# First attention: both halves' logits in a row, the values' products behind them, ScalarE's turned copies between the second half's exponentials

## The chip, the cores and the metric

The kernel runs on one core of a Trainium2 chip. The core has a matmul engine (TensorE, PE in the profile; its weight loads are shown apart as PEld), VectorE (DVE), ScalarE (ACT), GpSimd (POOL) and SyncE (SP), which issues most of the transfers. Each engine takes its own instructions in the order in which they are written, and waits for the others on semaphores. The metric is the device time of one execution in microseconds (us); lower is better.

## The reference

A small vision tower over 16 images of 36 patches and one class token each, so 37 tokens per image, 592 in all, 256 features wide, float32 throughout. Six stages follow each other: patch embedding, a first attention, a mixture of experts, a second attention with three iterations, and a feed-forward stage with quantised weights. The change is in the first attention alone:

```python
q = (x @ Wq.T + bq) * 16 ** -0.5          # 16 heads of 16
kv = x @ Wkv.T + bkv                       # one key and one value head for all
k, v = kv[..., :16], kv[..., 16:]
qr = q.reshape(B, 16 * 37, 16)
probs = softmax(qr @ k.T, axis=-1)         # (B, 592, 37)
out = (probs @ v)  # laid back to (B, 37, 256)
h = h + out @ Wo.T + bo
```

## The kernel before

The whole kernel is written as one instruction stream per engine. The 16 images are treated in two halves `u` of eight images. For each half the first attention goes through these steps:

- Logits: `attention_scores(u)` on TensorE (L1944) fills four banks `("S", u, j)`, one for each two images. A product has 16 rows of contraction and 37 columns, and four of them lie side by side in the array. 80 matmul instructions make one half.
- Softmax: `scores(u, j)` on VectorE takes the maximum (L1263) and writes logits less maximum into `probs`, which lies in the tile `big` (L1264); that empties the bank. `exps(u, j)` on ScalarE takes the exponential in place (L798). `row_sums(u, j)` on VectorE sums and inverts (L1270, L1271). GpSimd multiplies by the inverse (L629) and counts up `probs_ready`.
- Turning: TensorE's `probs_turned(u)` waits for all four multiplications of the half and turns the probabilities by 15 matmuls with the identity into five banks `("PT", u, t)` (L1958). They are copied to `probsT[u]`, which is `cur` for half 0 and `probs` for half 1: half 0 by ScalarE (L803), half 1 by ScalarE and VectorE in turn (L803, L1276).
- Output: `attention_values(u)` on TensorE (L1975, 128 matmuls) waits for all five copies and for `vals_ready`. ScalarE's `heads_out` (L808) takes the result to `att`, and `project` (L1756) multiplies by the output weights.

The values themselves come from `values_of_tokens()` on TensorE (24 matmuls into the bank `("v0",)`, recorded at L1756 as `bank<-wkvT,xT`), `values()` on VectorE (L1293 to L1298), which adds the bias, and `values_by_slot()` on GpSimd (L618), which spreads them over slots and counts up `vals_ready`.

There are eight PSUM banks, and they are used strictly in turn. The list `fills()` names every filling of a bank in TensorE's order, and who empties it. TensorE may fill number n only when number n - 8 is emptied. Emptied banks are counted by one semaphore for each emptying stream (`act`, `dve`, `rates`), in the order of that engine's work, and `NTH` gives the count that a key has to wait for. So the list has to have the same order as the engine's program, within each semaphore.

Before the change TensorE's order in this stage is: logits of half 0, values' products, logits of half 1, turn half 0, outputs of half 0, turn half 1, first part of the projection, outputs of half 1, rest of the projection. ScalarE's order is: four exponentials of half 0, four of half 1, five copies of the turned half 0, `heads_out` of half 0, and so on. VectorE's is: four `scores` of half 0, `values()`, four `row_sums` of half 0, four `scores` of half 1, four `row_sums` of half 1. GpSimd's is: four multiplications of half 0, `values_by_slot()`, four multiplications of half 1.

Of the kernel before, what the change touches and what calls it, by code (L numbers as in the profile page):

```python
# [26 lines left out]
ALU = mybir.AluOpType  # L27
# [3 lines left out]
P = 128  # L31
B = 16
NG = 6
T = NG * NG + 1
# [15 lines left out]
RT = 5  # L50
# [40 lines left out]
def fills():  # L91

    def channel(c, gs=range(2)):
        f.extend((("xp", 2 * c + half, g), "act") for g in gs for half in range(2))

    f = [(("ln",), "act")]
    f.extend((("ad", t), "act") for t in range(TT))
    channel(0)
    f.append((("cs",), "act"))
    channel(1, (0,))  # L100
    f.append((("mr",), "act"))
    f.append((("cr",), "dve"))
    channel(1, (1,))
    channel(2)
    f.append((("rt",), "rates"))
    f.extend((("y", t), "dve") for t in range(TT))
    f.append((("wl",), "dve"))
    f.append((("wn",), "dve"))
    f.append((("bl",), "dve"))
    f.append((("bq",), "act"))  # L110
    f.extend((("wT", n), "act") for n in ("q0", "o0"))
    f.append((("wkvT",), "act"))
    for i in range(3):
        f.append((("xT", 0, i), "act"))
    f.append((("k0",), "dve"))
    for g in range(6):
        f.append((("q0", g), "act" if g % 2 else "dve"))
    for u in range(2):
        f.extend((("S", u, j), "dve") for j in range(4))
        if not u:  # L120
            f.append((("v0",), "dve"))
    for u in range(2):
        f.extend((("PT", u, t), "act" if u == 0 or t % 2 == 0 else "dve") for t in range(RT))
        if u:
            f.append((("wo", 0, 0), "dve"))
        f.extend((("PV", u, g), "act") for g in range(2))
    f.extend((("wo", 0, j), "dve") for j in range(1, 3))
    f.extend((key, "act") for key in (("pw", 0), ("wc", "q"), ("pw", 1), ("wc", 1), ("wc", 2), ("wc", 3), ("cst",)))
    for i in range(3):
        f.append((("xT", 1, i), "act"))  # L130
    f.extend((("lg", c), "act") for c in range(2))
    f.append((("lgT",), "act"))
    for e in range(NX + 1):
        if e < NX:
            for c in range(2):
                f.append((("g", e, c), "act"))
                f.append((("u", e, c), "dve"))
        if 1 <= e <= NE or e == NX:
            for i in range(3):
                f.append((("d", min(e - 1, NE), i), "dve"))  # L140
    f.extend((("fw", n), "dve" if n % 2 else "act") for n in range(6))
    f.extend((("wT", n), "act") for n in ("v1", "o1"))
    for i in range(3):
        f.append((("xT", 2, i), "dve" if i == 1 else "act"))
    us = range(2)
    f.extend((("nc", "k", 1, u), "act") for u in us)
    for u in us:
        f.append((("nc", "q", 1, u), "dve"))
        f.append((("nv", 1, u), "act"))
    f.extend((("nc", "k", 2, u), "act") for u in us)  # L150
    f.extend((("vt", u), "act") for u in us)
    for a in (1, 2, 3):
        f.append((("fS", a, 0), "dve"))
        f.append((("fV", a), "act"))
        f.append((("fS", a, 1), "dve"))
        if a == 1:
            f.extend((("vr", 0, j), "dve") for j in range(4))
            f.extend((("vr", 1, j), "act" if j < 2 else "dve") for j in range(4))
        else:
            f.extend((("out", a - 1, u), "act") for u in us)  # L160
        f.extend((("fPT", a, u), "act") for u in us)
        if a == 1:
            f.extend((("nv", 2, u), "act") for u in us)
        if a == 1:
            f.append((("nc", "k", 3, 0), "act"))
        if a == 3:
            f.append((("df",), "dve"))
        f.extend((("O", a, u), "dve") for u in us)
        if a == 1:
            f.append((("nc", "k", 3, 1), "act"))  # L170
        f.extend((("OT", a, u), "dve") for u in us)
        if a < 3:
            f.extend((("nc", "q", a + 1, u), "dve") for u in us)
        if a == 1:
            f.extend((("nv", 3, u), "act") for u in us)
    f.extend((("out", 3, u), "dve") for u in us)
    for i in range(3):
        f.append((("wo", 1, i), "dve"))
    f.extend((("fw", n), "act") for n in range(6, 9))
    for i in range(3):  # L180
        f.append((("xT", 3, i), "dve" if i == 1 else "act"))
    f.extend((("ga", o, c), "act") for o in range(FC) for c in range(2))
    f.append((("mx", 1), "dve"))
    f.extend((("up", c), "act") for c in range(len(UC)))
    f.extend((("mx", n), "dve") for n in (2, 3, 4))
    f.extend((("dn", t), "dve") for t in range(TT))
    return f
# [8 lines left out]
ROOTS.extend(("placed", _t) for _t in range(TT - 2, TT))  # L196
ROOT = {key: n + 1 for n, key in enumerate(ROOTS)}
NTH = {}
for _who in ("act", "dve", "rates"):
    for _n, _key in enumerate(k for k, w in FILLS if w == _who):  # L200
        NTH[_key] = (_who, _n + 1)

# [7 lines left out]
def build(nc, i, out):  # L210

    with ExitStack() as ctx:
# [3 lines left out]
        def sem(name):  # L216
            return ctx.enter_context(nc.semaphore(name))
# [180 lines left out]
        banks = [ctx.enter_context(nc.psum_tensor(f"bank{n}", [P, 512], F32)) for n in range(8)]  # L398

        bank_filled = sem("bank_filled")  # L400
        emptied_by = {"act": sem("act_emptied"), "dve": sem("dve_emptied"), "rates": sem("rates_emptied")}
        dve_chain, act_chain, pool_chain = sem("dve_chain"), sem("act_chain"), sem("pool_chain")
        images_in = [sem(f"images_in{n}") for n in range(NC)]
        (patch_w_in, ln_in, norm_rows_in, cols_in, small_w_in, attn_w_in, rows_in, pos_in, moe_in, ffn_in, out_stored) = (
# [139 lines left out]
        def _(pool):  # L544
# [68 lines left out]
            def values_by_slot():  # L613

                pool.wait_ge(attn_cleared, 3)
                pool.wait_ge(values_in, 1)
                for h_ in range(2):
                    ins = pool.tensor_tensor(vals[0:G3, :, :, h_, h_ * HD:(h_ + 1) * HD],  # L618
                                             vb[:, :, :].unsqueeze(2).to_broadcast([G3, 6, 3, HD]),
                                             slot_of[:, :].unsqueeze(1).unsqueeze(3).to_broadcast([G3, 6, 3, HD]), ALU.mult)  # L620
                ins.then_inc(vals_ready, 1)

            for u in range(2):
                if u:
                    values_by_slot()
                for j in range(4):
                    pool.wait_ge(sums_ready, 4 * u + j + 1)
                    v = probs[:, u, :, 2 * j:2 * j + 2, :]
                    pool.tensor_tensor(v, v, row_sum[:, u, j].unsqueeze(3).to_broadcast([P, RT, 2, T]),  # L629
                                       ALU.mult).then_inc(probs_ready, 1)  # L630
            filled(pool, ("wo", 0, 2))
            pool.memset(att[:, :], 0.0).then_inc(attT_cleared, 1)

# [59 lines left out]
        def _(act):  # L693
# [101 lines left out]
            def exps(u, j):  # L795
                emptied(act, ("S", u, j))
                v = probs[:, u, :, 2 * j:2 * j + 2, :]
                act.activation(v, v, ACT.Exp).then_inc(exp_done, 1)  # L798

            def probs_turned(u, t):  # L800
                b = take(act, ("PT", u, t))
                n = min(P, R - t * P)
                empty(act.copy(probsT[u][:, :, t * P:t * P + n], b[0:G3, 0:3 * P].rearrange("p (g r) -> p g r", g=3)[:, :, 0:n]))  # L803
# [6 lines left out]

            for j in range(4):
                exps(0, j)
            for j in range(4):
                exps(1, j)
            for t in range(RT):
                probs_turned(0, t)
            for g in range(2):
                heads_out(0, g)
            for t in range(0, RT, 2):
# [192 lines left out]
        def _(dve):  # L1012
# [275 lines left out]
            def values():  # L1288

                b = take(dve, ("v0",))[:, 0:6 * HD].rearrange("p (u g d) -> p u g d", u=2, g=3)  # L1290
                bv = bv_row[:, :].unsqueeze(1).unsqueeze(1)
                v = vb.rearrange("p (u g) d -> p u g d", u=2)
                link(dve.memset(vb[64:G3, :, :], 0.0))  # L1293
                link(dve.tensor_tensor(v[:, :, 0:2, :], b[0:G3, :, 0:2, :], bv[0:G3].to_broadcast([G3, 2, 2, HD]), ALU.add))
                ins = dve.tensor_tensor(v[0:2 * T, :, 2, :], b[0:2 * T, :, 2, :],
                                        bv_row[0:2 * T, :].unsqueeze(1).to_broadcast([2 * T, 2, HD]), ALU.add)
                empty(ins)
                dve.tensor_copy(first[:, 0:1], ident[0:T, 0:1]).then_inc(values_in, 1)  # L1298

            for j in range(4):  # L1300
                scores(0, j)
            values()
            for j in range(4):
                row_sums(0, j)
            for j in range(4):
                scores(1, j)
            for j in range(4):
                row_sums(1, j)
# [423 lines left out]
        def _(pe):  # L1732
# [258 lines left out]
            for g in range(6):  # L1991
                emptied(pe, ("q0", g))
            attention_scores(0)
            values_of_tokens()
            attention_scores(1)

            probs_turned(0)
            attention_values(0)
# [284 lines left out]
```

## Time and profile before

| what | value |
|---|---|
| time, median of three runs | 292.12 us (292.08 to 292.67) |
| the profiled execution's own time | 292.1 us |
| its span, first to last instruction | 290.4 us |
| mean granted TensorE clock over the span | 0.929 of full |
| PE busy, DVE busy, ACT busy, POOL busy | 88%, 70%, 35%, 20% |
| the first attention, from its first logits to the end of its projection | 52.5 to 83.9 us |

The profiled execution is a normal one: its time lies inside the three runs. 1.7 us of it lie outside the span. The rows of the next section come from this execution; all places in them are microseconds from the span's start.

### The profile page before, as it was taken

The numbers are of one execution on the slowest core, as the hardware profiler recorded it, in microseconds if no ns is written. First come the engines' busy times: TensorE is split into PE (matmuls) and PEld (weight loads), VectorE is DVE, ScalarE is ACT, GpSimd is POOL, SyncE is SP. The second block draws the span as 40 slices with busy tenths as digits, with TensorE's granted clock in tenths as the row PEclk, the third lists the DMA queues.
The fourth block names the chain that finished last, engine by engine and source line by source line (L and its number), as shares of the span: only waits on it lengthen the run. The fifth ranks groups of instructions, "written<-read, shape, count | busy, mean of one in ns | idle before, by whom it ended". The sixth has DMA issues, their size and how long they took to land.

```text
span 290.4 us, 5610 instructions
## 1 busy us (share of the span) xinstructions
PE 254.6 (88%) x2199; PEld 208.9 (72%) x2199; DVE 201.9 (70%) x483; ACT 101.1 (35%) x243; POOL 58.4 (20%) x117
## 2 busy tenths in 40 slices
PE   5999989896999999999999799988788999745696
PEld 4888879795986677877777587866566776434584
DVE  2884866487532697888979667856878548987831
ACT  2571352115325511111112564672304337444000
POOL 8770540054012000000000144992000000000000
PEclk9988979757899999999999999999899999969599
DMA  7949540000005300000000000000000000000011
GB/s 202 270 129 282 154 166 5 2 2 2 2 2 180 146 2 0 0 0 2 0 1 0 2 0 2 3 0 2 2 3 0 0 0 2 0 0 1 0 36 47
DMA packets 14471, 12.01 MB, mean 41 GB/s; under 512 B 2995, under 2 KB 13902, under 8 KB 14446
## 3 DMA queue, kind: packets, MB, share of 16 engines
q1 hardware_dynamic: 14376, 11.62, 13.5%
q8 instruction: 17, 0.28, 0.4%
q10 hardware_dynamic: 70, 0.05, 0.1%
q14 instruction: 8, 0.07, 0.1%
HBM read 11.05 MB, written 0.61 MB: 40 GB/s over the span
## 4 chain that ended last, share of the span: by engine, by line
PE 70%; DVE 18%; ACT 7%; issue 3%; POOL 1%; ACTq 0%; DVEq 0%; POOLq 0%
PE bank L1756 46%; PE bank L1838 5%; PE bank L2250 5%; PE bank L1911 3%; PE bank L1944 3%; DVE part L1600 2%; PE bank L1975 2%; PE bank L1751 2%; DVE big L1664 1%; DVE keys_n L1645 1%; PE bank L1886 1%; DVE big L1698 1%; ACT big L1002 1%; PE bank L1783 1%; ACT xT L776 1%
## 5 line engine op out<-in xcount | busy, mean ns | idle before, releaser
L1756 PE MATMUL bank<-xT,big 128*128 128x296 f32 (+1 forms) x192 | 45.7, 391 | 0.0
L1756 PEld LDWEIGHTS bank<-xT,big 128*128 128x128 f32 x192 | 34.3, 190 | 9.5 <-issue 0.2
L1756 PE MATMUL bank<-xT,fT 128*128 128x296 f32 (+12 forms) x96 | 24.6, 416 | 0.6 <-DVE xT L1621 0.6
L853 ACT ACTIVATE cen<-bank 128x296 f32<-128x296 f32 x20 | 8.3, 418 | 46.4 <-PE bank L1756 40.7
L1756 PE MATMUL bank<-big,cur 128*128 128x256 f32 (+1 forms) x100 | 23.3, 381 | 0.7 <-DVE cur L1375 0.7
L1751 PE MATMUL bank<-ident,ones 128*128 128x128 f32 x104 | 18.0, 340 | 5.3 <-POOL rsd L559 3.5
L1756 PEld LDWEIGHTS bank<-xT,fT 128*128 128x128 f32 x96 | 17.2, 191 | 7.1 <-issue 2.1
L1756 PEld LDWEIGHTS bank<-big,cur 128*128 128x128 f32 (+1 forms) x100 | 18.0, 182 | 4.9 <-DVE cur L1375 1.5
L1751 PEld LDWEIGHTS bank<-ident,ones 128*128 128x128 f32 x104 | 16.8, 249 | 5.8 <-POOL rsd L559 3.5
L1388 DVE SCALAR_TENSOR_TENSOR h<-bank,route,h 128x256 f32<-128x256 f32 (+1 forms) x40 | 17.0, 478 | 2.9 <-PE bank L1756 2.9
L669 POOL TENSOR_SCALAR big<-keys_n,k_w 128x256 f32<-128x256 f32 x24 | 17.5, 748 | 4.8 <-DVE keys_n L1479 4.8
L1600 DVE TENSOR_REDUCE part<-big 128x1 f32<-128x296 f32 (+2 forms) x18 | 13.1, 731 | 6.3 <-ACT big L989 6.3
L661 POOL COPY cur<-xT 128x256 f32<-128x256 f32 x2 | 0.7, 402 | 72.3 <-ACT xT L778 72.3
L2250 PE MATMUL bank<-fT,big 128*128 128x256 f32 (+1 forms) x60 | 14.7, 410 | 0.5 <-DVE big L1597 0.5
L1838 PE MATMUL bank<-small,big 128*128 128x256 f32 (+1 forms) x60 | 14.9, 415 | 0.0
L2250 PEld LDWEIGHTS bank<-fT,big 128*128 128x128 f32 (+1 forms) x60 | 11.9, 201 | 3.2 <-DVE big L1597 0.8
L1838 PEld LDWEIGHTS bank<-small,big 128*128 128x128 f32 (+1 forms) x60 | 12.0, 202 | 2.4
L1375 DVE TENSOR_TENSOR cur<-cen,bank 128x296 f32<-128x296 f32 x20 | 9.1, 461 | 4.8 <-PE bank L1756 4.4
L1756 PE MATMUL bank<-wT_o,att 128*128 128x256 f32 (+1 forms) x40 | 9.3, 383 | 1.5 <-DVE att L1556 0.9
L629 POOL TENSOR_TENSOR big<-big,row_sum 128x370 f32<-128x370 f32 x8 | 6.2, 811 | 20.6 <-DVE row_sum L1271 20.6
L2220 PE MATMUL bank<-ident,mx 128*128 128x128 f32 x4 | 1.7, 422 | 9.4 <-DVE mx L1603 5.6
L1756 PEld LDWEIGHTS bank<-wT_o,att 128*128 128x128 f32 (+1 forms) x40 | 7.0, 182 | 3.1 <-DVE att L1556 1.3
(325 smaller groups left out, 514.9 us busy)
## 6 DMA issues: line engine op xcount, KB each, us to landing
big<-in_x SPq DMA_DIRECT2D x3, 576.0 KB, 7.6
big<-in_L_ffn_w_gate SPq DMA_DIRECT2D x2, 512.0 KB, 6.8
big<-in_L_ffn_w_up SPq DMA_DIRECT2D x2, 512.0 KB, 6.8
big<-in_L_ffn_w_down SPq DMA_DIRECT2D x1, 1024.0 KB, 5.5
small<-in_L_tok_lin_w SPq DMA_DIRECT2D x3, 256.0 KB, 5.4
small<-in_L_ffn_w_gate SPq DMA_DIRECT2D x1, 768.0 KB, 4.6
small<-in_L_ffn_w_up SPq DMA_DIRECT2D x1, 768.0 KB, 6.9
small<-in_L_ffn_w_down SPq DMA_DIRECT2D x1, 768.0 KB, 8.2
```

What stands on the lines that cost most here:

```text
L629: pool.tensor_tensor(v, v, row_sum[:, u, j].unsqueeze(3).to_broadcast([P, RT, 2, T]), ALU.mult).then_inc(probs_ready, 1)
L669: ins = pool.tensor_scalar(fkeys[a - 1][:, u, :, n, :], keys, k_w[:, a - 1, n:n + 1], 1.0, ALU.mult, ALU.mult)
L853: empty(act.activation(silu[:, c, :], b[:, 0:HP], ACT.Silu))
L1375: empty(dve.tensor_tensor(hid[:, e % 3, c * HP:(c + 1) * HP], silu[:, c, :], b[:, 0:HP], ALU.mult))
L1388: ins = dve.scalar_tensor_tensor(out=v, in0=src, scalar=route[0:n, t, e:e + 1], in1=v, op0=ALU.mult, op1=ALU.add)
L1600: return dve.tensor_reduce(part[:, n:n + 1], v, AX.X, ALU.max, apply_absolute_value=True)
L1751: pe.matmul(b[:, 0:P], ones[:, :], ident[:, :], start=True, stop=True)
L1756: ins = pe.matmul(out_, a_, b_, start=(n == 0), stop=(n == len(pairs) - 1))
L1838: ins = pe.matmul(b[0:rows, 0:D], patT[:, k, t * P:t * P + rows], lin_w[:, k, :], start=(k == 0), stop=(k == PK - 1))
L1911: ins = pe.matmul(b[32 * j:32 * j + m, at_:at_ + 4 * T].rearrange("p (u c) -> p u c", u=2), w(k), xq[:, k, :, 2 * j * T:2 * (j + 1) * T], ...
L1944: ins = pe.matmul(bs_[j][:, (2 * t + s) * T:(2 * t + s + 1) * T], qT[rows, row:row + P], kT[rows, u, s * T:(s + 1) * T], start=True, stop= ...
L2250: ins = pe.matmul(b[0:rows, 0:D], gate[:, o * NT + t * P:o * NT + t * P + rows], fT[2][:, o, :], start=(o == 0), stop=(o == FC - 1))
```

## The change

TensorE makes the logits of both halves without a break and the values' products after them. VectorE does the sums of half 0, two of the second half's `scores`, then `values()`, then the other two `scores`. GpSimd spreads the values after the four multiplications of half 0, as before, but this is now written out. ScalarE puts the five copies of the turned half 0 between the four exponentials of half 1. The bank of the values gets a semaphore of its own (`values`), because the place of `values()` in VectorE's program is no longer the place of its bank in the order of fills. The number of instructions that compute stays as it was on every engine.

```diff
@@ fills()
-    for u in range(2):
-        f.extend((("S", u, j), "dve") for j in range(4))
-        if not u:
-            f.append((("v0",), "dve"))
+    f.extend((("S", u, j), "dve") for u in range(2) for j in range(4))
+    f.append((("v0",), "values"))
@@ GpSimd
-            for u in range(2):
-                if u:
-                    values_by_slot()
-                for j in range(4):
-                    ...
+            for j in range(4):
+                normalised(0, j)
+            values_by_slot()
+            for j in range(4):
+                normalised(1, j)
@@ ScalarE
             for j in range(4):
                 exps(0, j)
-            for j in range(4):
-                exps(1, j)
-            for t in range(RT):
-                probs_turned(0, t)
+            exps(1, 0)
+            probs_turned(0, 0)
+            exps(1, 1)
+            probs_turned(0, 1)
+            probs_turned(0, 2)
+            exps(1, 2)
+            probs_turned(0, 3)
+            exps(1, 3)
+            probs_turned(0, 4)
@@ VectorE, values()
-                empty(ins)
+                ins.then_inc(emptied_by["values"], 1)
@@ VectorE
             for j in range(4):
                 scores(0, j)
-            values()
             for j in range(4):
                 row_sums(0, j)
-            for j in range(4):
+            for j in range(2):
+                scores(1, j)
+            values()
+            for j in range(2, 4):
                 scores(1, j)
             for j in range(4):
                 row_sums(1, j)
@@ TensorE
             attention_scores(0)
+            attention_scores(1)
             values_of_tokens()
-            attention_scores(1)
```

## Rows read from the trace of the kernel before

**Rows 1.** The page: share of the chain by engine.

```profile
PE 70%; DVE 18%; ACT 7%; issue 3%; POOL 1%; ACTq 0%; DVEq 0%; POOLq 0%
```

**Rows 2.** The chain that ended last, 51 to 92 us: start, length, what.

```profile
64.11 0.54 DVE row_max L1263
...
68.32 0.52 ACT big L798
68.84 1.78 ACT cur L803 x5
70.61 0.24 issue
70.85 3.82 PE bank L1975 x128
```

**Rows 3.** TensorE's timeline: start, length, what, times, idle before and who ended it.

```profile
55.46 4.18 PE L1756 MATMUL bank<-wkvT,xT 128*111 128x16 f32 x24
59.57 4.50 PE L1944 MATMUL bank<-kT,qT 16*128 16x37 f32 x80
64.57 3.48 PE L1958 MATMUL bank<-ident,big 128*111 128x128 f32 x15 [0.50 <-POOL big L629]
70.85 3.82 PE L1975 MATMUL bank<-cur,small 111*32 111x74 f32 x128 [2.80 <-ACT cur L803]
74.60 1.93 PE L1958 MATMUL bank<-ident,big 128*111 128x128 f32 x15
76.37 1.89 PE L1756 MATMUL bank<-wT_o,att 128*128 128x256 f32 x8
78.19 2.27 PE L1975 MATMUL bank<-probs,small 111*32 111x74 f32 x128
```

**Rows 4.** Windows: stretch, length, busy time of PE, PEld, DVE, ACT, POOL, granted clock, transfers.

```profile
51.40:54.20 2.80, 1.67 (x60) 1.70 (x61) 0.46 (x1) 0.51 (x1) 0.00 (x0) 1.00 0.03 6
54.30:67.80 13.50, 13.00 (x144) 12.73 (x141) 10.74 (x28) 3.59 (x7) 4.37 (x6) 0.50 0.00 1
67.90:71.20 3.30, 0.50 (x22) 0.38 (x25) 2.88 (x9) 2.28 (x6) 2.14 (x3) 1.00 0.00 0
71.40:74.60 3.20, 3.20 (x107) 3.00 (x100) 0.00 (x0) 0.41 (x1) 0.78 (x2) 0.50 0.03 5
...
190.80:194.20 3.40, 2.26 (x38) 1.59 (x37) 2.05 (x5) 2.11 (x9) 3.39 (x7) 1.00 0.00 0
194.20:197.60 3.40, 2.80 (x68) 2.16 (x68) 3.25 (x7) 2.29 (x10) 3.40 (x5) 1.00 0.02 5
```

**Rows 5.** VectorE's timeline around the two halves' softmax.

```profile
59.13 0.54 DVE L1264 TENSOR_TENSOR big<-bank,row_max 128x370 f32<-128x370 f32 x1
...
60.35 0.52 DVE L1270 TENSOR_REDUCE row_sum<-big 128x10 f32<-128x370 f32 x1
...
62.84 0.22 DVE L1271 RECIPROCAL row_sum<-row_sum 128x10 f32<-128x10 f32 x1
64.08 0.54 DVE L1263 TENSOR_REDUCE row_max<-bank 128x10 f32<-128x370 f32 x1 [1.02 <-PE bank L1944]
...
67.74 0.55 DVE L1264 TENSOR_TENSOR big<-bank,row_max 128x370 f32<-128x370 f32 x1
68.20 0.53 DVE L1270 TENSOR_REDUCE row_sum<-big 128x10 f32<-128x370 f32 x1
```

**Rows 6.** ScalarE's timeline, same stretch.

```profile
68.32 0.52 ACT L798 ACTIVATE big<-big 128x370 f32<-128x370 f32 x1 [0.52 <-DVE big L1264]
68.74 1.86 ACT L803 COPY cur<-bank 111x384 f32<-111x384 f32 x5
```

**Rows 7.** GpSimd's timeline, same stretch.

```profile
61.20 3.12 POOL L629 TENSOR_TENSOR big<-big,row_sum 128x370 f32<-128x370 f32 x4 [17.15 <-DVE row_sum L1271]
64.28 1.29 POOL L618 TENSOR_TENSOR small<-vb,slot_of 111x288 f32<-111x288 f32 x2
69.06 3.12 POOL L629 TENSOR_TENSOR big<-big,row_sum 128x370 f32<-128x370 f32 x4 [3.49 <-DVE row_sum L1271]
```

More of the change, by code:

```diff
@@ L198 @@
 NTH = {}
-for _who in ("act", "dve", "rates"):
+for _who in ("act", "dve", "rates", "values"):
     for _n, _key in enumerate(k for k, w in FILLS if w == _who):
@@ L400, in build @@
         bank_filled = sem("bank_filled")
-        emptied_by = {"act": sem("act_emptied"), "dve": sem("dve_emptied"), "rates": sem("rates_emptied")}
+        emptied_by = {"act": sem("act_emptied"), "dve": sem("dve_emptied"), "rates": sem("rates_emptied"),
+                      "values": sem("values_emptied")}
         dve_chain, act_chain, pool_chain = sem("dve_chain"), sem("act_chain"), sem("pool_chain")
@@ L621, in values_by_slot, with normalised @@
                 ins.then_inc(vals_ready, 1)
-            for u in range(2):
-                if u:
-                    values_by_slot()
-                for j in range(4):
[L627 to L630, printed above, removed]
+            def normalised(u, j):
+                pool.wait_ge(sums_ready, 4 * u + j + 1)
+                v = probs[:, u, :, 2 * j:2 * j + 2, :]
+                pool.tensor_tensor(v, v, row_sum[:, u, j].unsqueeze(3).to_broadcast([P, RT, 2, T]),
+                                   ALU.mult).then_inc(probs_ready, 1)
+            for j in range(4):
[3 more added lines that the diff above has]
+                normalised(1, j)
             filled(pool, ("wo", 0, 2))
```

## The prediction

> **What bounds the kernel now.** I read the page first: TensorE holds most of the chain that ended last [rows 1]. That is a mean over six stages, so I went to the chain in the first attention [rows 2]. There TensorE does not set the end throughout. At 64.11 the chain leaves it for VectorE, which takes the second half's maxima and subtractions until ScalarE has its last exponential at 68.32. Then come ScalarE's five copies of the turned half 0 to 70.61, and only then TensorE's outputs of half 0 at 70.85. TensorE's timeline shows the hole from its own side: its turning ends at 68.05, and it sits idle 2.80 us until ScalarE's copies are there [rows 3]. The bank copied first was full near 65.5 (three of the fifteen transposes), and ScalarE took it at 68.74 [rows 6]. ScalarE was not short of time: it idled 0.52 us before its last exponential, and its own order kept the copies behind it [rows 6].
>
> The granted clock comes next [rows 4]. From 54.3 to 67.8 it is 0.50, the level of 1.2 GHz: logits, values' products and turning. From 67.9 to 71.2 it is 1.00, 2.4 GHz, and there TensorE works only 0.50 of 3.30 us. From 71.4 to 74.6 it is 0.50 again, and TensorE works all of it. So the outputs of half 0 take 3.82 us, and the same 128 instructions for half 1, at full clock, 2.27 us [rows 3]. Ahead of the rise stood the transposes of half 0; ahead of the fall the hole.
>
> **The change part by part.**
>
> *TensorE: logits together, values' products last.* The two pieces that change places fill 55.46 to 64.07 without a hole, at half clock throughout [rows 3, 4]. In either order they are done by about 63.9; I take no gain and no loss (bounds 63.8 and 64.1). The logits of half 1 are then ready near 60.0, where VectorE waited 1.02 us for them until 64.08 [rows 5]. All eight banks are in use, so turning copies 3 and 4 now wait for the first two `scores` of half 1 (63.3 and 64.3, below), and are reached at 65.9 and later. That costs nothing.
>
> *VectorE.* `values()` costs 0.76 us: 1.22 us from the last subtraction (59.13) to the first sum (60.35), less the 0.46 us between such instructions where nothing is between them (67.74 to 68.20) [rows 5]. New order: sums of half 0 from 59.59, four in 2.62 us (60.35 to 63.06, less a small overlap), to 62.21. One `scores` is 4.12 / 4 = 1.03 us (64.08 to 68.20). Two of them reach 64.27, `values()` 65.03, two more 67.09. The sums of half 1 thus start 1.11 us sooner than at 68.20. Their cover: the values' products must be full by 64.3 and are at about 63.9. Past that margin of 0.4 us each tenth goes into all that follows.
>
> *GpSimd.* Half 0's multiplications come 0.76 us sooner, 60.44 to 63.56. The first transpose began 0.25 us after their end (64.32 to 64.57) [rows 3, 7], which gives 63.81. TensorE is free at about 63.9, so turning half 0 starts at 63.9 in place of 64.57. `values_by_slot()` now stands in front of half 1's multiplications with its wait for `values()`: 65.1 to 66.4 (1.29 us), while their first sum comes near 67.9. It has 1.5 us of cover, and the outputs need it only at 68.3. Half 1's multiplications come with VectorE, 1.11 us sooner: 67.95 to 71.07.
>
> *ScalarE.* A copy follows a copy after 0.37 us (1.86 for five), an exponential (0.52 us) is followed by a copy after 0.42 us [rows 6]. The transposes are 3.48 / 15, about 0.22 us apart and 0.42 us long, so the banks are full at 64.8, 65.4, 66.1, 66.7, 67.4. The `scores` of half 1 are done at 63.3, 64.3, 66.1, 67.2. In ScalarE's order: exponential 0 at 63.4, copy 0 at 64.8, exponential 1 at 65.2, copy 1 at 65.6, copy 2 at 66.1, exponential 2 at 66.5, copy 3 at 66.9, exponential 3 at 67.3, copy 4 at 67.7 to 68.1. With the 0.24 us of issue [rows 2] the outputs of half 0 start at 68.3 in place of 70.85. The copies now block exponentials in one queue. Queued behind exponential 3 are VectorE's fourth sum of half 1 (due 67.09 + 3 * 0.65 = 69.0) and behind that GpSimd. Exponential 3 ends at 67.8, so 1.2 us hide it.
>
> *What the earlier outputs gain.* They start where the clock was at full. Turning half 0 is still the work ahead of 67.8 (63.9 to 67.3 in place of 64.57 to 68.05), so I let the clock rise there as before. Outputs of half 0: 68.3 + 2.27 = 70.6. Turning half 1 then waits for GpSimd: 71.07 + 0.25 = 71.3 in place of 74.60. This is the term that counts, 3.3 us. The hole does not vanish: some 0.7 us of it now stands in front of that turning, and GpSimd's chain (VectorE's sums, in the end the `scores`) is late next.
>
> *Bounds on the outputs.* At half clock they take at most 3.82 us [rows 3] and end at 72.1. At full clock they are 2.27 us and hidden by the wait for GpSimd. I take 2.27.
>
> *After 71.3.* Turning half 1 takes 1.77 us to the projection (74.60 to 76.37), its first tenth at half clock; I take 0.1 us off. This needs full clock past 71.3, where it fell before. Before the fall TensorE had worked 0.50 of 3.30 us. Now it works some 2.3 of the same stretch. The nearest rows: 190.8 to 194.2, with 2.26 of 3.40 us of work and a hole of 1.2 us, and the clock stayed full to 197.6; against 51.4 to 54.2, with 1.67 of 2.80 us, all of it 16-row logits, and the clock fell [rows 4]. The outputs are like the first in share and in shape (32 array columns, as that stretch's logits and products have), so I take full clock.
>
> Everything later (projection, expert weights' composition, routing, experts) hangs on TensorE's chain and moves as a block, transfers of the last stage's weights with it, since they are issued on a bank of that chain. The new semaphore adds no instruction that computes: 0.
>
> Sum: 3.3 + 0.1 = 3.4 us off a span of 290.4 is 287.0; the profiled execution's 292.1, which is the median of the runs shown, becomes 288.7 us.
>
> *A rule against it.* The rows show the clock rise from 0.50 to 1.00 at about 67.8, with TensorE on nothing but the transposes of half 0 since 64.57 [rows 3, 4]. The Trainium skill, "TensorE: Matmul & The Clock Gate", section "Part 4: PE-mode transpose", says that the full clock doesn't engage for transposes. By that rule the outputs of half 0 would run at half clock, and the sum would be that of rival 2; the trace disagrees, as the clock rose right behind them.
>
> **Rivals.**
>
> 1. *The clock falls at 71.3 after all.* For: it fell exactly there before, and TensorE still has two holes in the stretch, of 0.5 and 0.7 us. Against: [rows 4] as above. Turning half 1 then takes about 3.48 in place of 1.93 us [rows 3]: gain 3.4 - 1.55 = 1.85, 290.3 us. If it stays down into the projection, up to 1.7 us more is lost (eight products of 1.89 us at full clock), which ends within measurement of no change.
>
> 2. *The clock does not rise at 67.8*, because turning ends 0.5 us before it now. Outputs end at 72.1, and turning half 1 starts at 72.15. At full clock: gain 2.45, 289.7 us. At half: 1.55 less, 291.2 us.
>
> 3. *ScalarE's queue becomes the bound; the change hardly does what it says.* If turning half 0 comes over 1.2 us later than 63.9, each copy holds an exponential and VectorE's sums with it. At 2 us late, GpSimd and turning half 1 are 0.8 us late, outputs run into the stretch after 71.3, and the gain is some 1.5 us: 290.6 to 291.6 us. For: one queue, four new places of waiting on TensorE. Against: the margins above.
>
> 4. *Slower: half clock over dense work.* A fall that is not lifted soon, as from 54.3 to 67.8 [rows 4], over the dense projection and compositions behind 71.3. Half clock takes twice the time of full, so each microsecond of it costs half a microsecond. It decides from 6.8 us of half clock on, where 3.4 us are lost; 13.5 us of it as there cost 6.75, which gives 292.1 - 3.4 + 6.75 = 295.4 us. Against: after 71.4 dense work at half clock brought full clock by 74.8.
>
> **How the numbers follow.** Forecast 0.62 (own range 288.2 to 289.2), rival 1 0.18, rival 2 0.07, rival 3 0.08, rival 4 0.05. The range goes from 287.9 (PE, VectorE and GpSimd bounds all at their good end, 0.8 us better) to 290.9 (rival 1 and a little more); outside are rival 4, most of rival 3, the bad end of 2, some 0.15 together. A measurement of this kernel can tell about 0.2%, 0.6 us. Faster by more: 0.62 + 0.18 + 0.06 + 0.04 = 0.90. Within: 0.05, from rivals 1, 2 and 3 at their ends. Slower: 0.05, rival 4.
>
> **What would show it.** In the profile after: logits of half 1 right behind half 0's and VectorE without a wait before 64; `values()` near 64.3 without a wait; ScalarE's last copy ending near 68.1; outputs of half 0 at 68.3 in about 2.3 us; turning half 1 near 71.3, released by GpSimd; granted clock 1.00 from 67.9 on. Wrong if TensorE's outputs of half 0 take near 3.8 us, if turning half 1 takes 3.5 us, if ScalarE waits for TensorE with exponentials behind it and VectorE waits for ScalarE, or if a new stretch at half clock stands later than 75.

## The result, and the profile after

| kernel | median | range | runs | ratio to the kernel before, 95% interval |
|---|---|---|---|---|
| before | 292.5 us | 291.95 to 294.8 | 20 | |
| changed | 289.38 us | 288.61 to 292.1 | 20 | 0.9894 [0.9872, 0.9915] |

Medians and ranges here are over all runs, while the ratios leave out the few runs of later batches that lie over 1.5% above the fastest of their kernel. The change makes the kernel 3.1 us faster (292.5 less 289.38), 1.1%; the interval of the ratio stands for 2.5 to 3.7 us. The forecast was 288.7 us against 292.1, which is 3.4 us less. The profiled execution of the changed kernel is one of its slower ones, 291.87 us with a span of 290.1: only 0.2 us less than before. So there are two things to read: the first attention, where the gain has to be, and what lies behind it.

TensorE's timeline of the changed kernel in the first attention (start, length, what, times, idle before and who ended it; compare [rows 3]; lines have moved by a few numbers):

```profile
52.66 7.17 PE L1953 MATMUL bank<-kT,qT 16*128 16x37 f32 x160 [1.15 <-ACT qT L793]
59.76 4.18 PE L1765 MATMUL bank<-wkvT,xT 128*111 128x16 f32 x24
63.86 3.51 PE L1967 MATMUL bank<-ident,big 128*111 128x128 f32 x15
68.30 2.27 PE L1984 MATMUL bank<-cur,small 111*32 111x74 f32 x128 [0.93 <-ACT cur L805]
71.30 1.86 PE L1967 MATMUL bank<-ident,big 128*111 128x128 f32 x15 [0.73 <-POOL big L625]
73.00 1.89 PE L1765 MATMUL bank<-wT_o,att 128*128 128x256 f32 x8
...
77.67 2.83 PE L1765 MATMUL bank<-wT_o,att 128*128 128x256 f32 x12 [0.56 <-ACT att L810]
```

The reader should see three things. The outputs of half 0 start at 68.30 in place of 70.85 and take 2.27 us in place of 3.82. Turning half 1 starts at 71.30 in place of 74.60, and GpSimd released it. The rest of the projection starts at 77.67, where the kernel before has 81.04 (an entry of its TensorE timeline of the same shape, `x12`): 3.37 us gained. ScalarE's timeline shows why the outputs could start:

```profile
63.36 0.51 ACT L800 ACTIVATE big<-big 128x370 f32<-128x370 f32 x1 [3.09 <-DVE big L1271]
64.85 0.48 ACT L805 COPY cur<-bank 111x384 f32<-111x384 f32 x1 [0.97 <-PE bank L1967]
65.22 0.52 ACT L800 ACTIVATE big<-big 128x370 f32<-128x370 f32 x1
65.64 0.97 ACT L805 COPY cur<-bank 111x384 f32<-111x384 f32 x2
66.50 0.52 ACT L800 ACTIVATE big<-big 128x370 f32<-128x370 f32 x1
66.92 0.47 ACT L805 COPY cur<-bank 111x384 f32<-111x384 f32 x1
67.28 0.53 ACT L800 ACTIVATE big<-big 128x370 f32<-128x370 f32 x1
67.69 0.36 ACT L805 COPY cur<-bank 111x240 f32<-111x240 f32 x1
```

From the first copy on ScalarE works without a hole, and the last copy ends at 68.05 in place of 70.60 [rows 6]. VectorE never waits for a logit of half 1 and starts its sums at 67.08 in place of 68.20 [rows 5]. GpSimd follows it to 71.05.

To compare executions a mark inside the stage is needed. VectorE's first maximum serves, since it is the first thing that VectorE does with the logits. The kernel before, then the changed one:

```profile
55.48 0.54 DVE L1263 TENSOR_REDUCE row_max<-bank 128x10 f32<-128x370 f32 x1 [3.62 <-PE bank L1944]
55.52 0.54 DVE L1270 TENSOR_REDUCE row_max<-bank 128x10 f32<-128x370 f32 x1 [3.54 <-PE bank L1953]
```

From there to the rest of the projection the kernel before takes 25.56 us (55.48 to 81.04) and the changed one 22.15 us (55.52 to 77.67), 3.4 us less.

The windows of the same execution (columns as in [rows 4]) show where the gain was lost again:

```profile
54.30:67.80 13.50, 13.07 (x150) 12.68 (x145) 11.69 (x31) 5.50 (x13) 4.40 (x6) 0.51 0.00 1
68.20:71.20 3.00, 2.27 (x128) 2.12 (x128) 1.49 (x6) 0.82 (x2) 2.85 (x4) 1.00 0.02 5
71.40:74.60 3.20, 3.20 (x23) 2.93 (x23) 2.29 (x4) 1.32 (x3) 0.00 (x0) 1.00 0.00 0
88.70:91.90 3.20, 3.02 (x6) 0.79 (x7) 0.00 (x0) 0.88 (x4) 0.84 (x5) 0.50 1.02 353
163.80:167.00 3.20, 3.20 (x17) 3.20 (x17) 0.00 (x0) 0.47 (x1) 0.37 (x2) 0.50 0.00 0
```

The granted clock rises ahead of the outputs and no longer falls behind them. But two new stretches at half clock (0.50) stand at 88.7 and 163.8. What they cost can be read off the same instructions in both kernels. The first two rows are of the kernel before, the other two of the changed one:

```profile
92.24 2.32 PE L1756 MATMUL bank<-xT,gate_w 128*8 128x320 f32 x8 [0.64 <-ACT xT L776]
165.53 2.05 PE L1756 MATMUL bank<-xT,wT_k 128*128 128x128 f32 x16 [1.07 <-ACT xT L778]
```

```profile
88.88 3.85 PE L1765 MATMUL bank<-xT,gate_w 128*8 128x320 f32 x8 [0.63 <-ACT xT L778]
163.52 3.61 PE L1765 MATMUL bank<-xT,wT_k 128*128 128x128 f32 x16 [0.92 <-ACT xT L780]
```

The router's logits took 1.53 us more and the second attention's first key products 1.56 us more. That is 3.1 us, nearly the whole gain. Idle time before them is the same or less, so nobody made them wait; they ran slower. In this execution the two stretches hide the change. Of the 20 runs 12 lie at 288.6 to 289.6 us, five at 290.5 to 291.0 and three, this one among them, at 291.8 to 292.1; what the clock did in the others was not recorded place by place.

### The profile page after: what moved, and what is told of

Its sections match the earlier page's. It is cut to its first block, busy times and chain, and to the rows that moved or that the text cites. A ratio compares the mean times of both kernels' runs of the same rounds, so it can differ in the third digit from the quotient of the medians.

```text
span 290.1 us, 5610 instructions
## 1 busy us (share of the span) xinstructions
PE 255.3 (88%) x2199; PEld 208.9 (72%) x2199; DVE 201.7 (70%) x483; ACT 100.9 (35%) x243; POOL 58.5 (20%) x117
## 4 chain that ended last, share of the span: by engine, by line
PE 67%; DVE 21%; ACT 6%; issue 3%; POOL 2%; ACTq 0%; DVEq 0%; POOLq 0%
PE bank L1765 46%; PE bank L2259 5%; PE bank L1847 5%; PE bank L1920 3%; DVE part L1609 2%; PE bank L1760 2%; DVE big L1271 1%; DVE big L1673 1%; DVE row_max L1270 1%; DVE keys_n L1654 1%; POOL big L625 1%; PE bank L1895 1%; PE bank L1953 1%; DVE big L1707 1%; ACT big L1009 1%
```

## The experiments

All medians below are of one batch each; the kernel before was run beside each of them. "Changed kernel" is the base for all variants but two, which start from the kernel before. Since the granted clock falls at other places from one execution to the next, a profile is read by the distances inside it, and the time by the ratio and its interval.

**The changed kernel again.**

> The changed kernel once more, as the base of this batch. Both theories: a gain of 3.1 us by the median. If the gain at the first attention (3.4 us) is fixed and the rest varies with where the granted clock falls later, the profile shows turning of half 1 at 71.3 us again, and the span lies at 287.0 plus about 1.5 us for each stretch at half clock between 85 and 204 us. If instead the late loss is fixed work added by the change, those stretches are there in every profile and the span is 290.1 again.

Measured: median 289.55 us, ratio 0.9915 [0.9879, 0.9951]. Its profile has a span of 287.8 us, where the expected sum (287.0 and 1.5 for one stretch) gives 288.5. Turning of half 1 again starts 3.01 us after the outputs of half 0 (67.51 to 70.52). The places are 0.8 us earlier than in the first profile, so the expected 71.3 was met only as a distance. Of the two late stretches only the second is there: the router's logits ran at full clock (2.32 us), the key products at half.

```profile
L1765 PE MATMUL bank<-xT,wT_k x16: 414/421/422, 161.2 to 164.4; 128*128 128x128 f32 x16
```

(Nanoseconds shortest/median/longest of one, first and last start; at full clock a key product takes 275 ns.) A third time, as the base of the last batch:

> The changed kernel a third time, as the base of this batch: median 289.4 to 289.6 us, turning of half 1 3.0 us after the start of the outputs of half 0.

Measured: median 289.51 us, ratio 0.9921 [0.9882, 0.996]; 68.52 to 71.52 is again 3.00 us. Here neither of the two late stretches occurred: the key products took 275 ns.

```profile
L1765 PE MATMUL bank<-xT,wT_k x16: 274/275/352, 162.2 to 164.0; 128*128 128x128 f32 x16
```

But the clock was at half elsewhere, from 203.8 to 207.2, over products of the second attention's last iteration. The same products in the kernel before, then in this execution (at full clock they take 2.02 us, as in the changed kernel's first profile):

```profile
207.07 3.04 PE L1756 MATMUL bank<-small,fprobsT 128*32 128x128 f32 x64
203.76 3.60 PE L1765 MATMUL bank<-small,fprobsT 128*32 128x128 f32 x64
```

So the gain in the first attention is fixed and the late loss is not. From VectorE's first maximum to the rest of the projection the three profiles take 22.15, 22.14 and 22.15 us. Of the two late stretches the first has both, the second one, the third none, but the third has another one, and so has the kernel before. With that one counted, the expected sum gives 288.5 us for the third, and its span is 288.5.

**Without ScalarE's new order.**

```diff
-            exps(1, 0)
-            probs_turned(0, 0)
-            ...
-            exps(1, 3)
-            probs_turned(0, 4)
+            for j in range(4):
+                exps(1, j)
+            for t in range(RT):
+                probs_turned(0, t)
```

> The change without ScalarE's new order: four exponentials of half 1, then the five copies. Forecast's theory (the copies' place in ScalarE's queue sets the outputs of half 0): copies from 67.7 to 69.5, outputs at 69.7 in place of 68.3; turning of half 1 at 72.0 if the clock stays full at 71.3 (gain 2.7 us against the kernel before), and a gain of 1.3 us if the longer hole lets it fall there. Rival (the new order of logits and values alone gives the gain, ScalarE's queue has slack): outputs at 68.3 and the same time as the changed kernel.

Measured: median 292.21 us, ratio 0.9964 [0.9925, 1.0004], not clear of no change. TensorE's timeline of this variant:

```profile
63.02 3.51 PE L1962 MATMUL bank<-ident,big 128*111 128x128 f32 x15 [0.30 <-POOL big L625]
68.89 3.74 PE L1979 MATMUL bank<-cur,small 111*32 111x74 f32 x128 [2.36 <-ACT cur L805]
72.56 1.89 PE L1962 MATMUL bank<-ident,big 128*111 128x128 f32 x15
```

The hole ahead of the outputs is 2.36 us (0.93 with the new order), and the outputs run at half clock, 3.74 us: the clock did not rise after the turning but only near 72.0, 0.6 us before the outputs end. The rival fails in the profile: the outputs come 5.87 us after the turning, not 4.44. The account of the clock was off: I had full clock for the outputs, and perhaps a fall behind them. The gain is 1.3 us at the rest of the projection (24.27 us from VectorE's first maximum, in place of 25.56) and 1.1 us by the ratio, near the lower of the two expected numbers (1.3 and 2.7), though its clock came about in another way.

**ScalarE's new order alone**, in the kernel before (the edit of the diff in ScalarE's program and nothing else).

> ScalarE's new order alone in the kernel before; TensorE, VectorE and GpSimd as before. Forecast's theory: copies between the exponentials end at 69.1 in place of 70.6, outputs of half 0 start at 69.35, mostly at full clock; turning of half 1 waits for GpSimd until 72.4 in place of 74.6: gain 2.2 us, or about 1.0 us if the clock falls at 71.3. Rival (without earlier logits of half 1 the copies only delay exponentials): turning of half 1 no earlier than 74, gain under 0.6 us.

Measured: median 291.53 us, ratio 0.9964 [0.9923, 1.0004], again not clear of no change; the ratio stands for 1.1 us, with an interval from a loss of 0.1 to a gain of 2.2.

```profile
65.14 3.51 PE L1963 MATMUL bank<-ident,big 128*111 128x128 f32 x15 [0.50 <-POOL big L629]
69.90 4.17 PE L1980 MATMUL bank<-cur,small 111*32 111x74 f32 x128 [1.25 <-ACT cur L803]
74.00 2.07 PE L1963 MATMUL bank<-ident,big 128*111 128x128 f32 x15
```

The hole shrank from 2.80 to 1.25 us, as expected, and the outputs started 4.76 us after the turning in place of 6.28 (64.57 to 70.85 [rows 3]). But they ran at half clock to the end, 4.17 us, so turning of half 1 started at 74.00, 8.86 us after that of half 0 in place of 10.03; nothing waited for GpSimd. Place 74 is what the rival had named, but not for its reason: the copies did come sooner, and the clock took it back. Half clock stood from 54 to 74.3:

```profile
54.00:74.30 20.30, 18.55 (x289) 17.83 (x288) 13.72 (x36) 6.31 (x15) 7.46 (x10) 0.50 0.01 2
```

Put together, in us from VectorE's first maximum (`row_max`) of each profile:

| kernel | start of the outputs of half 0 | their own time | start of the rest of the projection |
|---|---|---|---|
| before | 15.37 | 3.82 | 25.56 |
| changed, without ScalarE's new order | 14.20 | 3.74 | 24.27 |
| before, with ScalarE's new order alone | 13.85 | 4.17 | 24.53 |
| changed, three profiles | 12.78, 12.77, 12.79 | 2.27, 2.26, 2.26 | 22.15, 22.14, 22.15 |

The starts of the outputs add up: 1.2 and 1.5 us from the parts, 2.6 from both. The gains behind them do not, 1.3 and 1.0 against 3.4, because each part by itself leaves the outputs at half clock in its profile. With both parts they took 2.26 to 2.28 us in all eight profiles, the three here and those of the five variants below that keep both. Whether a part alone meets full clock in other executions is not seen. Its runs reach down to 289.5 us, but so do two runs of the kernel before in this batch (289.79 and 289.86).

**Dummies ahead of the outputs, in the kernel before**: the clock without any reordering.

```diff
+                b = fill(("PV", u, 0))
+                if u == 0:
+                    keep_awake(b, 10)
                 pe.wait_ge(vals_ready, 1)
                 for t in range(RT):
                     emptied(pe, ("PT", u, t))
...
-                    b = fill(("PV", u, x))
+                    if x:
+                        b = fill(("PV", u, x))
```

> The kernel before, with ten dummy products (ones by identity, 2.2 us at full clock) put into TensorE's hole ahead of the outputs of half 0; they go to the outputs' own bank, which is then overwritten. No order is changed. If part of the change's gain is the clock alone, the outputs of half 0 stay at full clock to their end, or fall less far: 2.3 to 2.9 us in place of 3.8, turning of half 1 1.0 to 1.5 us earlier, and the median 1.0 to 1.5 us under the kernel before. Rival (the clock only follows the place of the work, dummies don't hold it): outputs at 3.8 us and no gain, or a loss of some tenths.

Measured: median 291.32 us against 292.52 in its batch, ratio 0.9949 [0.9913, 0.9985]: 1.2 us by the medians and 1.5 by the ratio (0.4 to 2.5), with no order changed.

```profile
63.81 3.51 PE L1958 MATMUL bank<-ident,big 128*111 128x128 f32 x15 [0.50 <-POOL big L629]
67.11 3.64 PE L1751 MATMUL bank<-ident,ones 128*128 128x128 f32 x20
70.69 2.27 PE L1979 MATMUL bank<-cur,small 111*32 111x74 f32 x128
72.89 1.89 PE L1958 MATMUL bank<-ident,big 128*111 128x128 f32 x15
```

The outputs take 2.27 us. The dummies overran their hole, since half clock stood until 69.7 and they took 3.64 us in place of the expected 2.2: the outputs start 6.88 us after the turning in place of 6.28. Even so turning of half 1 starts 9.08 us after that of half 0, where the kernel before needs 10.03 (64.57 to 74.60). So about 1.5 us of the outputs' time was the clock. The profile holds a second finding. With the work 1.76 us earlier than before (79.28 in place of 81.04 at the rest of the projection), the same two late stretches fell to half clock, though this is the old order. The first line is the first attention, the other two the late stretches:

```profile
53.00:69.60 16.60, 16.10 (x166) 15.88 (x164) 13.20 (x35) 5.63 (x13) 5.65 (x8) 0.50 0.00 1
90.30:93.50 3.20, 3.01 (x6) 0.78 (x7) 0.00 (x0) 0.89 (x4) 0.83 (x5) 0.50 1.06 361
165.40:168.60 3.20, 3.20 (x17) 3.20 (x17) 0.00 (x0) 0.47 (x1) 0.40 (x2) 0.50 0.00 0
```

So these stretches do not need the new order. That an earlier place brings them on is not shown either: in the change without ScalarE's new order that stage started 2.1 us earlier than before (78.96), and both stretches ran at full clock.

**Dummies in the late holes of the changed kernel**, eight and twelve as in the edit, then two and four in their places.

```diff
             turn(1, 2)
             for c in range(2):
-                emptied(pe, ("xT", 1, 1 + c))
                 b = fill(("lg", c))
+                if c == 0:
+                    keep_awake(b, 8)
+                emptied(pe, ("xT", 1, 1 + c))
...
-            turn(2, 3)
+            turn(2, 3, awake=12)
```

> The changed kernel, with dummy products of the ones and the identity put into two idle holes of TensorE: eight ahead of the router's logits, twelve at the start of the turning ahead of the second attention. The dummies go to banks that are then overwritten. If the late loss is the granted clock (router's logits 3.85 us at half clock in place of 2.32, first products of the second attention at half clock), both stretches run at full clock in the profile, the span is near 287.0, the median near 288.8 and the spread of the runs becomes smaller. Rival (the loss comes from transfers or from other engines that the shift brought together): the same median as the changed kernel or up to 1 us more, for the dummies.

Measured: median 290.53 us, ratio 0.9922 [0.9885, 0.996]. The granted clock is 1.00 over all of 68 to 254 us, as the theory wants, but the median is 1.0 us over the changed kernel's of the same batch, which is the rival's number. The span is 288.7 us, not 287.0. The doses are too large: from the rest of the projection to the first expert took 15.58 us (14.50 in the changed kernel's second profile, with the same products at full clock), from there to the second attention 71.06 (69.84 there). That is 2.3 us for dummies, which the expected 288.8 us had left out. The runs lie closer together, as expected: 289.46 to 291.8 us, against 288.5 to 292.26 (and one at 294.19) for the changed kernel beside them. So the profile speaks for the clock, but the time shows no gain.

> As the variant with eight and twelve dummies, but with two ahead of the router's logits and four ahead of the turning before the second attention, so that they fit the idle holes of 0.63 and 0.92 us. The larger doses cost 1.1 us each. If the doses fit, the two stretches take 14.5 us (end of the first attention to the first expert) and under 61.8 us (second attention to the last stage's first products), and the median is 0.5 to 1.5 us under the changed kernel. Rival (small doses don't hold the clock): no change, or 0.2 us lost.

Measured: median 288.97 us in six runs, ratio 0.9846 [0.9798, 0.9894]. The two stages took 14.50 and 69.85 us, so the doses cost nothing. From the key products to the last stage's first products it took 61.52 us (under 61.8 expected; 62.85 in the changed kernel's second profile), and the key products ran at full clock. The dummies in their place ahead of the router's logits:

```profile
86.14 1.29 PE L1895 MATMUL bank<-ident,xn 128*128 128x128 f32 x10
87.27 0.61 PE L1760 MATMUL bank<-ident,ones 128*128 128x128 f32 x4
88.07 2.32 PE L1765 MATMUL bank<-xT,gate_w 128*8 128x320 f32 x8 [0.19 <-ACT xT L778]
```

The idle 0.63 us ahead of the router's logits is down to 0.19, and they take 2.32 us. The median is 0.6 us under the changed kernel's 289.55 of the batch before; the intervals of the two overlap. That the doses hold the clock is not shown: the changed kernel's third profile has these two stretches at full clock without any dummies. And like that profile this one is at half clock from 203.4 to 206.8 (products of 3.15 in place of 2.02 us).

**GpSimd's chain.** The last of half 1's four multiplications on VectorE.

```diff
-            for j in range(4):
+            for j in range(3):
                 normalised(1, j)
...
+            last = probs[:, 1, :, 6:8, :]
+            dve.tensor_tensor(last, last, row_sum[:, 1, 3].unsqueeze(3).to_broadcast([P, RT, 2, T]),
+                              ALU.mult).then_inc(probs_ready_dve, 1)
...
+                if u:
+                    pe.wait_ge(probs_ready_dve, 1)
```

> The changed kernel, with the last of half 1's four multiplications by the inverse sums moved from GpSimd to VectorE, with a semaphore of its own. Forecast's theory (GpSimd's chain is late next and makes the 0.7 us hole ahead of turning half 1): the hole closes, turning of half 1 starts 2.3 us after the outputs of half 0 in place of 3.0, and the median is 0.6 to 0.7 us under the changed kernel. Rival (another wait takes its place or the clock falls): same time as the changed kernel.

Measured: median 289.64 us in six runs, ratio 0.9887 [0.9832, 0.9943]: no gain that the median shows, though with six runs and the changed kernel only in other batches 0.6 us could not be told. In the profile turning of half 1 starts 2.64 us after the outputs in place of 3.00:

```profile
67.34 2.26 PE L1993 MATMUL bank<-cur,small 111*32 111x74 f32 x128 [1.00 <-ACT cur L806]
69.98 1.86 PE L1976 MATMUL bank<-ident,big 128*111 128x128 f32 x15 [0.39 <-DVE big L1323]
```

```profile
68.88 0.85 DVE L1323 TENSOR_TENSOR big<-big,row_sum 128x370 f32<-128x370 f32 x1
```

The hole is halved and its releaser is now VectorE's multiplication, which took 0.85 us, where a subtraction of the same size takes 0.54 [rows 5]. That is 0.3 of the 0.39 us that are left of it.

**The values after all four subtractions.**

```diff
-            for j in range(2):
-                scores(1, j)
-            values()
-            for j in range(2, 4):
+            for j in range(4):
                 scores(1, j)
+            values()
```

> The changed kernel, with VectorE's treatment of the values after all four subtractions of half 1 in place of the middle of them. By the margins of the forecast: GpSimd's spreading of the values starts at 67.1 in place of 65.2 and ends at 68.4, so its multiplications of half 1 start 0.5 us later and turning of half 1 with them; outputs of half 0 start 0.2 to 0.4 us later. Cost 0.5 us against the changed kernel. Rival (the place of the values does not matter, 1.5 us of cover): no change.

Measured: median 290.44 us, ratio 0.9908 [0.9874, 0.9942]. From the turning of half 0 to that of half 1 it takes 8.06 us in place of 7.44 (63.86 to 71.30).

```profile
62.90 3.42 PE L1965 MATMUL bank<-ident,big 128*111 128x128 f32 x15
67.68 2.27 PE L1982 MATMUL bank<-cur,small 111*32 111x74 f32 x128 [1.36 <-POOL small L617]
70.96 1.86 PE L1965 MATMUL bank<-ident,big 128*111 128x128 f32 x15 [1.01 <-POOL big L625]
```

Both waits are now GpSimd's: its spreading of the values is the last thing the outputs wait for, 0.34 us later after the turning than in the changed kernel (4.78 and 4.44 us), and its multiplications come later. The step costs 0.6 us in the profile, against 0.5 expected; the median lies 0.9 us over the 289.5 that the changed kernel has in the other batches.

**Both small additions.** Shared multiplication and small doses.

> The changed kernel with both: the last multiplication of half 1 on VectorE, and two and four dummies in the holes. The shared multiplication gave turning of half 1 0.35 us earlier against the outputs of half 0, the small doses some 0.5 us in the median. If they add, the median is 0.8 to 0.9 us under the changed kernel of the same batch, near 288.6 us. Rival (0.35 us shifts the rest against the clock and costs as much again): the same as with the dummies alone, 289.0 us.

Measured: median 288.76 us against 289.51 for the changed kernel of the same batch, ratio 0.9889 [0.9854, 0.9924] to the kernel before. That is 0.75 us by the medians, near the expected sum, but the interval holds the changed kernel's ratio of 0.9921 too. It is the lowest median of all, and not clearly a better kernel than the changed one. Its profile too has the last iteration's products at half clock (3.62 us from 201.91).

## Why the prediction was right

- *The hole and who makes it.* Right. Forecast for the outputs of half 0: 68.3; measured 68.30. Last copy ending at 68.1; measured 68.05. The variant with the old order of ScalarE has the hole back (2.36 us). Of the 2.55 us by which the outputs start sooner ScalarE's order is worth about 1.5 and the other engines' order about 1.2.
- *Logits and values' products change places at no cost.* Right: turning of half 0 started at 63.86, forecast 63.9.
- *VectorE's 1.11 us and the 0.76 us of `values()`.* Right: sums of half 1 from 67.08, forecast 67.09. No wait for the values' products.
- *GpSimd late next.* Right: it released turning of half 1 at 71.30, forecast 71.3, after a hole of 0.73 us. Moving one multiplication away closed half of the hole; delaying GpSimd by the place of the values cost 0.6 us.
- *Full clock for the outputs.* Right in all eight profiles with the whole change. The outputs start 2.55 us sooner and take 1.55 us less, and the new hole of 0.73 us takes part of that back, which makes the 3.3 us at the turning of half 1. The dummies in the old order show that the clock alone gives about 1.5 us there; in the new order the hole would have covered 0.7 us of its loss. The reason given, that the turning is still the work ahead of the rise, is not enough, and this part owes something to luck. In the first profile half clock ended at 68.1, 0.2 us ahead of the outputs (in the others between 65.4 and 67.2). In both variants with one part the clock stayed at half behind the same turning, through the outputs (3.74 and 4.17 us). The place of the turning alone does not decide it: without ScalarE's new order it ran from 63.02, in the variant with small doses from 63.03, and there half clock ended at 66.9. What decides stays open. The bound of rival 2 was too low as well: "at most 3.82 us" was read from outputs that had begun at full clock, and wholly at half clock they took 4.17.
- *Rival 1, a fall at 71.3.* Did not happen in any of the eight; turning of half 1 took 1.86 us. That half clock "takes twice the time of full" (rival 4) is a little high by the rows: the outputs take 4.17 and 2.27 us, the 15 transposes 3.51 and 1.86, which is 1.8 and 1.9 times.
- *The rule that transposes don't bring the full clock* (the Trainium skill, "TensorE: Matmul & The Clock Gate", section "Part 4: PE-mode transpose"): the clock was full by 68.2 with nothing but transposes on TensorE since 63.86, as before. The trace disagrees with the page for these float32 transposes. It is no rule that they bring the full clock either: behind the same 15 it stayed at half in both variants with one part, and in the old order with dummies it rose only at 69.7, under the dummies.
- *"Everything later moves as a block."* Right for the order and the waits, and silent on the clock. At the rest of the projection the gain is 3.37 us of the forecast 3.4. In the profiled execution 3.1 us were then lost at two places of half clock. I had looked at the clock behind the change only as one long fall (rival 4, 6.8 us of half clock) and not at short stretches around the idle holes of TensorE. By the sign that the prediction named, "a new stretch at half clock stands later than 75", this profile counts against it, and the time of that execution, 291.87 us, lies outside its range. The runs show that such stretches belong neither to the new order nor to this kernel: the kernel before has one at 207.8, the old order with dummies the same two as the changed kernel, and the changed kernel's other two profiles one each. Their cost to the median was not measured: 3.1 us of gain against 3.4 is a difference inside the interval of 2.5 to 3.7. Which executions get which stretch stays open.
- *The number.* 289.38 us is inside the range of 287.9 to 290.9 and just above the forecast's own range of 288.2 to 289.2. Of the 0.7 us between it and 288.7, 0.4 is the starting point (292.1 from three runs, 292.5 from twenty), and 0.3 the gain. The good end of the range, 0.8 us better, was given without a sum.

## What to carry to other kernels

When an engine's queue holds copies that could go long ago behind work that is not yet possible, put them in between, but do it together with whatever makes the blocked work possible: here the two halves' gains in the profile were 1.3 and 1.0 us and the whole 3.4, and neither half alone was clear of no change by its ratio. Read the granted clock at the place where the moved work will land, since it can be a large part of the gain (outputs 1.55 us shorter here, of 3.3 us). And look at unchanged stages further down as well: they can run at another clock in the one execution that is profiled, before or after, so that one profile can show none of the gain that twenty runs show.

## What the runs showed that I had not expected

The places at which the granted clock changes are not tied to the program. In the variant with small doses the long stretch at half clock of the first attention began later, at 56.6: the logits of both halves took 4.96 us, against 7.17 in the changed kernel's first profile. Yet the outputs came 15.2 us after the first logit (52.26 to 67.46), against 15.64 (52.66 to 68.30):

```profile
52.26 4.96 PE L1953 MATMUL bank<-kT,qT 16*128 16x37 f32 x160 [1.15 <-ACT qT L793]
57.15 4.18 PE L1765 MATMUL bank<-wkvT,xT 128*111 128x16 f32 x24
63.03 3.51 PE L1967 MATMUL bank<-ident,big 128*111 128x128 f32 x15 [1.70 <-POOL big L625]
67.46 2.28 PE L1984 MATMUL bank<-cur,small 111*32 111x74 f32 x128 [0.93 <-ACT cur L805]
```

TensorE there waited 1.70 us for GpSimd. So in that stretch VectorE, GpSimd and ScalarE set the pace. From VectorE's first maximum to the outputs it takes 12.77 us in this profile and 12.77 to 12.79 in the three of the changed kernel, whether the logits take 4.96 or 7.91 us. What the clock of the logits changes is when VectorE starts: 2.43 us after the first logit here, 2.86 and 3.58 us in the changed kernel's first two profiles. TensorE also fell to half clock with work on it ahead of the fall: 1.75 of 3.20 us from 162.0 to 165.2 in the old order with dummies, half clock from 165.4 on.
